# Query projection of the 16-head cross-attention as three fp16 passes, weights split on GpSimd

## The reference

```python
q = (text_hidden @ Wq).reshape(B, T_text, 16, 128).transpose(0, 2, 1, 3)
k = (vision_tokens @ Wk).reshape(B, T_vis, 8, 128).transpose(0, 2, 1, 3)
v = (vision_tokens @ Wv).reshape(B, T_vis, 8, 128).transpose(0, 2, 1, 3)
# k and v are repeated for the two heads of a group
scores = jnp.einsum('bhtd,bhsd->bhts', q, k) / scale
attn = jax.nn.softmax(jnp.where(mask, scores, -jnp.inf), axis=-1)
out = jnp.einsum('bhts,bhsd->bhtd', attn, v)  # then the heads side by side
return out @ Wo
```

## Time and profile before

| what | value |
|---|---|
| median of the runs | 1304.71 us (1302.49 to 1308.16) |
| the profiled execution's own time | 1302.72 us |
| its span | 1301.0 us |
| TensorE busy | 1152.5 us, 89% |
| VectorE busy | 994.7 us, 76% |
| ScalarE busy | 860.9 us, 66% |
| GpSimd busy | 315.3 us, 24% |
| the projection's matmuls (line 442) | 192 records |

### The profile page before, as it was taken

The page is one execution under the profiler, slowest core; times in us unless marked ns, Lnnn a source line. Parts: engine busy times, 40 slices in busy tenths (PEclk is TensorE's granted clock), DMA queues, the critical chain, the costliest instruction groups (busy, mean ns, idle before and its releaser), DMA issues. The chain is left out here.

```text
span 1301.0 us, 23119 instructions
## 1 busy us (share of the span) xinstructions
PE 1152.5 (89%) x8740; PEld 765.0 (59%) x8744; DVE 994.7 (76%) x1866; ACT 860.9 (66%) x1303; POOL 315.3 (24%) x353
## 2 busy tenths in 40 slices
PE   7999999848776887799899999887998999999997
PEld 3677767635322444486566666645874666666654
DVE  6887788197768883593889989776987998998654
ACT  5787778484454887332777777565876777777563
POOL 3000000100362000000172654502650456265100
PEclk8999999959986999899899999999998999999989
DMA  7999989201374000901899999614745999999600
GB/s 279 181 187 189 189 166 192 70 1 73 84 144 81 2 3 2 232 36 59 152 198 183 206 184 168 124 54 157 206 115 129 180 181 185 177 164 163 122 1 9
DMA packets 450833, 170.00 MB, mean 131 GB/s; under 512 B 437160, under 2 KB 437544, under 8 KB 449064
## 3 DMA queue, kind: packets, MB, share of 16 engines
q1 hardware_dynamic: 450736, 168.72, 62.3%
HBM read 58.84 MB, written 0.26 MB: 45 GB/s over the span
## 5 line engine op out<-in xcount | busy, mean ns | idle before, releaser
L462 PE MATMUL ps<-ctxT,L_xattn_qk 128*128 128x512 f16 x1152 | 269.4, 384 | 0.8 <-DVE L_xattn_mx L742 0.5
L766 DVE SCALAR_TENSOR_TENSOR arena<-L_xattn_sm,L_xattn_rr,arena 128x1024 f16<-128x1024 f32 x192 | 260.5, 1398 | 9.4 <-ACT arena L612 9.4
L597 ACT ACTIVATE L_xattn_sm<-L_xattn_sm,L_xattn_mx 128x2048 f32<-128x2048 f32 x96 | 192.3, 2003 | 74.9 <-DVE L_xattn_mx L742 73.5
L612 ACT ACTIVATE arena<-L_xattn_sm,L_xattn_rr 128x1024 f16<-128x1024 f32 x192 | 210.0, 1140 | 5.2
L462 PEld LDWEIGHTS ps<-ctxT,L_xattn_qk 128*128 128x128 f16 x1152 | 112.3, 99 | 129.4 <-issue 8.9
L484 PE MATMUL ps<-arena,ctx 128*128 128x256 f16 x1488 | 177.6, 273 | 0.0
L484 PEld LDWEIGHTS ps<-arena,ctx 128*128 128x128 f16 x1488 | 145.4, 98 | 31.9
L742 DVE CUSTOM_DVE_ANT_0 L_xattn_sm<-ps,L_xattn_bias 128x1024 f32<-128x1024 f32 x96 | 117.1, 1220 | 55.0 <-issue 54.7
L742 DVE CUSTOM_DVE_ANT_0 L_xattn_sm<-ps,L_xattn_bias,L_xattn_mx 128x1024 f32<-128x1024 f32 x96 | 123.2, 1284 | 2.0 <-DVE L_xattn_mx L742 1.3
L475 PE MATMUL ps<-arena,ctx 128*128 128x128 f16 x1488 | 100.8, 222 | 9.7 <-DMA arena<-arena 9.5
L475 PEld LDWEIGHTS ps<-arena,ctx 128*128 128x128 f16 x1488 | 92.3, 99 | 25.1 <-DMA arena<-arena 13.3
(11 more groups left out here) (586 smaller groups left out, 2094.2 us busy)
## 6 DMA issues: line engine op xcount, KB each, us to landing
L_ffn_ring<-in_L_ffn_experts SPq DMA_DIRECT2D x34, 384.0 KB, 3.7
arena<-in_L_xattn_w SPq DMA_DIRECT2D x36, 320.0 KB, 3.7
arena<-in_L_ffn_experts SPq DMA_DIRECT2D x8, 768.0 KB, 8.6
arena<-in_L_xattn_w SPq DMA_DIRECT2D x6, 640.0 KB, 8.5
arena<-arena SPq DMA_TRANSPOSE x193, 4.5
arena<-in_L_ffn_codes SPq DMA_DIRECT2D x1, 3072.0 KB, 12.2
arena<-in_L_attn_w SPq DMA_DIRECT2D x1, 2163.0 KB, 19.1
arena<-in_L_attn_w SPq DMA_DIRECT2D x2, 1026.0 KB, 5.0
```

Of the source, the lines that this page charges most:

```text
L462: last = nc.tensor.matmul(ps[:, at, :], qk[:, h // 2, qp, h % 2, b * P:(b + 1) * P], k.ctxT[:, cp, b, at * 512:(at + 1) * 512], start=(a = ...
L597: nc.scalar.activation(sm[:, u % 2, :], sm[:, u % 2, :], ACT.Exp, bias=mx[:, u % 2, 1:2], scale=-1.0, accum_out=rs[:, u % 2:u % 2 + 1]).th ...
L612: nc.scalar.mul(pp[:, u % 2, 0, at], sm[:, u % 2, at], rr[:, u % 2:u % 2 + 1]).then_inc(s.p_high, 1)
L766: nc.vector.scalar_tensor_tensor(pp[:, u % 2, 1, at], sm[:, u % 2, at], rr[:, u % 2:u % 2 + 1], pp[:, u % 2, 0, at], ALU.mult, ALU.subtrac ...
```

## The change

The query projection of the three layers is computed in three fp16 passes. Its two factors are split:

- The norm. ScalarE copies the turned norm from PSUM as fp16 (the high part), then VectorE subtracts that from PSUM into a second fp16 tile (the low part). Both lie in the memory of `k.xnT`, as `xh`. TensorE waits for the low part (`xn_low`).
- The weights. GpSimd copies a group's Wq to fp16 and subtracts (`split_queries`), into a new tile `wqh` with two places. TensorE waits for `wq_low` where it waited for the load. The wait for the load moves to GpSimd, which also waits until the projection that last read the place is done.

`q_project` issues 12 matmuls instead of 4. In L0_xattn GpSimd splits the first two groups around its subtractions and all others after them, as their weights arrive. In L2_xattn and L3_xattn it splits groups (0, 0) and (0, 1) before the first expert; the split of (i+1, 0) stands between the scalings and the clips of expert i, that of (i+1, 1) behind the clips.

The diff, without its first hunk, which adds the semaphore `xn_low`:

```diff
--- before.py
+++ after.py
@@ -302,7 +302,7 @@
             return stack.enter_context(nc.sbuf_tensor(f"{name}_{nm}", shape, dt))
         s = semaphores(nc, stack, name, "wq0 wq1 wv0 wv1 out_done qT_psum qT_ready qk_psum qk_high qk_ready s_ready "
                  "s_read0 s_read1 p_ready r_raw r_ready p_high p_low t_hi0 t_hi1 t_lo0 t_lo1 mixed "
-                 "oT_ready oh_psum oh_ready mask_ready last_psum last_hi last_lo0 last_lo1 oT_low", k.turns[slot])
+                 "oT_ready oh_psum oh_ready mask_ready last_psum last_hi last_lo0 last_lo1 oT_low wq_low", k.turns[slot])
         w = k.arena[slot][:, 0:2 * GW].rearrange("p (a n) -> p a n", a=2)
         bias = sb("bias", [P, B, CTX], BF16)
         anyone = sb("anyone", [P, B])
@@ -314,6 +314,8 @@
         pp = k.arena[slot][:, 2 * GW + 2 * CTX:2 * GW + 4 * CTX].bitcast(F16).rearrange("p (s a n) -> p s a n", s=2, a=2)
         pt = k.arena[slot][:, 2 * GW:2 * GW + 2 * CTX].bitcast(F16)\
             .rearrange("p (s a t q) -> p s a t q", s=2, t=KT, a=2)
+        xh = flat(k.xnT[:]).bitcast(F16).rearrange("p (a c t) -> p a c t", a=2, c=DC)
+        wqh = sb("wqh", [P, 2, 2, 2 * DC * HD], F16)
         qT = sb("qT", [P, 2, T])
         qk = sb("qk", [P, 2, 2, 2, T], F16)
         mx = sb("mx", [P, 2, 2])
@@ -326,7 +328,7 @@
             weigh = Weigh(sb("round", [P, WE]), sb("exp", [P, FE // 2, WE // BLK]), sb("inv", [P, FE // 2, WE // BLK]))
         oT = sb("oT", [P, T])
         oh = sb("oh", [P, T])
-        wq = [w[:, i, 0:2 * DC * HD].rearrange("p (h c d) -> p h c d", h=2, c=DC) for i in range(2)]
+        wq = [wqh[:, i, :, :].rearrange("p a (h c d) -> p a h c d", h=2, c=DC) for i in range(2)]
         wkT = [w[:, i, 512:640] for i in range(2)]
         wv = [w[:, i, 640:768] for i in range(2)]
         wo = [w[:, i, 768:768 + 2 * D].rearrange("p (h d) -> p h d", h=2) for i in range(2)]
@@ -425,22 +427,19 @@
                 keep_busy(k, 1, 3 if opening else 4, still)
                 xT_tensor(k, pe, k.xn, 0, n)
                 keep_busy(k, 1, 5, still)
-                pe.wait_ge(g.xnT_ready, k.xt + 1)
+                pe.wait_ge(g.xn_low, {"L0_xattn": 1, "L2_xattn": 2, "L3_xattn": 3}[name])
 
                 def q_project(i, j, first):
 
-                    if first and opening:
-                        pe.wait_ge((g.first_w0, g.first_w1)[j], 16)
-                    elif first:
-                        wait_weights(k, pe, slot, loaded)
-                    else:
-                        pe.wait_ge(wq_sem[j], 16 * i)
+                    pe.wait_ge(s.wq_low, 2 * i + j + 1)
                     if not (first and j == 0):
                         pe.wait_ge(s.qk_ready, 2 * i + j)
                     for h in range(2):
                         for c in range(DC):
-                            last = nc.tensor.matmul(PREP[:, h * T:(h + 1) * T], wq[j][:, h, c, :], k.xnT[:, c, :],
-                                                    start=(c == 0), stop=(c == DC - 1))
+                            for a, (wpart, xp) in enumerate(PARTS):
+                                last = nc.tensor.matmul(PREP[:, h * T:(h + 1) * T], wq[j][:, wpart, h, c, :],
+                                                        xh[:, xp, c, :], start=(c == 0 and a == 0),
+                                                        stop=(c == DC - 1 and a == len(PARTS) - 1))
                     last.then_inc(s.qT_psum, 1)
 
                 def qk_project(i, j):
@@ -579,7 +578,8 @@
             @block.scalar
             def _(act):
                 ln_scalar(k, act, n)
-                xT_scalar(k, act, k.xnT, 0)
+                act.wait_ge(g.xnT_psum, k.xt + 1)
+                nc.scalar.copy(xh[:, 0, :, :].rearrange("p c t -> p (c t)"), ps[:, 0, :]).then_inc(g.xnT_ready, 1)
                 nc.scalar.activation(unused[:], k.zero[:], ACT.Exp, bias=k.zero[:])
 
                 def q_copy(i, j):
@@ -693,22 +693,48 @@
 
             @block.gpsimd
             def _(pool):
+                def split_queries(chain, i, j):
+
+                    if i == 0 and opening:
+                        pool.wait_ge((g.first_w0, g.first_w1)[j], 16)
+                    elif i == 0:
+                        wait_weights(k, pool, slot, loaded)
+                    else:
+                        pool.wait_ge(wq_sem[j], 16 * i)
+                        pool.wait_ge(s.qT_psum, 2 * i + j - 1)
+                    chain(nc.gpsimd.tensor_copy(wqh[:, j, 0, :], w[:, j, 0:2 * DC * HD]))
+                    nc.gpsimd.tensor_tensor(wqh[:, j, 1, :], w[:, j, 0:2 * DC * HD], wqh[:, j, 0, :], ALU.subtract)\
+                        .then_inc(s.wq_low, 1)
+
                 if opening:
                     constants_pool(k, pool)
+                chain = Chain(pool, g.pool_chain, k.pool_n)
+                split_queries(chain, 0, 0)
+                if opening:
                     for b, done in enumerate((g.values_high0, g.values_high1)):
+                        if b:
+                            split_queries(chain, 0, 1)
                         pool.wait_ge(done, 1)
                         for half in range(2):
                             at = slice(half * CTX // 2, (half + 1) * CTX // 2)
                             nc.gpsimd.tensor_tensor(rows_of(1, b)[:, at], raw_context(k, b)[1][:, at], rows_of(0, b)[:, at],
                                                     ALU.subtract).then_inc(g.values_low, 1)
-                if experts is not None:
-                    experts_pool(k, pool, weigh, experts)
+                    for i in range(1, LASTI + 1):
+                        for j in range(2):
+                            split_queries(chain, i, j)
+                else:
+                    split_queries(chain, 0, 1)
+                    experts_pool(k, pool, chain, weigh, experts, split_queries)
+                k.pool_n = chain.n
 
             @block.vector
             def _(dve):
                 if opening:
                     dve.wait_ge(g.x_loaded, 16)
                 ln_vector(k, dve, k.x, k.xn, LN_EPS, n)
+                dve.wait_ge(g.xnT_ready, k.xt + 1)
+                nc.vector.tensor_tensor(xh[:, 1, :, :].rearrange("p c t -> p (c t)"), ps[:, 0, :],
+                                        xh[:, 0, :, :].rearrange("p c t -> p (c t)"), ALU.subtract).then_inc(g.xn_low, 1)
                 if opening:
                     dve.wait_ge(g.mask_loaded, 16)
                 else:
@@ -3200,10 +3226,9 @@
     k.dve_n = chain.n
 
 
-def experts_pool(k, pool, w, first):
+def experts_pool(k, pool, chain, w, first, split_queries):
 
     nc, g = k.nc, k.g
-    chain = Chain(pool, g.pool_chain, k.pool_n)
     blocks = WE // PIECES // BLK
 
     for e in range(first, first + FE // 2):
@@ -3216,11 +3241,15 @@
         for j in range(PIECES):
             nc.gpsimd.tensor_tensor(in_blocks(y[j]), in_blocks(y[j]), each_block(inv[j]), ALU.mult)\
                 .then_inc(g.w_scaled, 1)
+        if e % 4 < LASTI:
+            split_queries(chain, e % 4 + 1, 0)
         pool.wait_ge(g.w_bits, e + 1)
         for j in range(PIECES):
             nc.gpsimd.tensor_scalar(y[j], y[j], E4M3_TOP, -E4M3_TOP, ALU.min, ALU.max)
             last = nc.gpsimd.tensor_scalar(r[j], r[j], E4M3_LOW, ROUND, ALU.max, ALU.mult)
         chain(last)
+        if e % 4 < LASTI:
+            split_queries(chain, e % 4 + 1, 1)
         shared = e % 4 == 3
         if shared:
             for j in range(PIECES // 2, PIECES):
@@ -3235,7 +3264,6 @@
         for j in own:
             nc.gpsimd.tensor_tensor(in_blocks(coded[j]), in_blocks(y[j]), each_block(ex[j]), ALU.mult)\
                 .then_inc(g.w_coded, 1)
-    k.pool_n = chain.n
 
 
 def turn_experts(k, sp, own):
```

More of the change, by code:

```diff
@@ L104, in begin @@
                                "keys_high0 keys_high1 keys_low0 keys_low1 values_high0 values_high1 values_low const_id const_zero const_ones const_copied "
-                               "var_ready std_ready xn_ready xnT_psum xnT_ready dve_chain act_chain pool_chain "
+                               "var_ready std_ready xn_ready xnT_psum xnT_ready xn_low dve_chain act_chain pool_chain "
                                "w_loaded0 w_loaded1 out_stored ln_chain "
```

## The result

The changed kernel took 1363.8 us (median of 4 runs, 1360.2 to 1367.8) against 1304.5 us before: 1.045 times as long, with a 95% interval of 1.041 to 1.050. Forecast were 1355 us, in a range of 1330 to 1370. The profiled execution took 1360.2 us, its span is 1358.4 against 1301.0, 57.4 us more.

The account below looks back on a forecast made before the run. TensorE was taken to bound the loops. From 1302.7 us: projections -8.5, starts +0.5, stalls +23.6 and +10.0, port +12.0, clock +13.0 gave 1353.3; 2.0 for the median made it 1355 us, range 1330 to 1370.

Parts of the forecast that it names:

- Stalls, 33.6 us bare: L2 and L3 loops: TensorE waits for GpSimd's queued weight splits, 23.6 us over six u = 2 and 10.0 over six u = 6.
- The port, 12.0 us: L2 and L3: VectorE's operations beside GpSimd's splits lengthen each of 12 splits by 1.0 us through shared SBUF access.
- the first place: TensorE's u = 2 in L2 and L3, where the split queued behind GpSimd's scalings was forecast 3.4 to 4.0 us late.
- rival A: L2 and L3: bare stalls, splits at their median times and the clock staying up; 1330 us, chance 0.20.
- The clock, 13.0 us: L2 and L3: TensorE's clock drops behind the six long stalls at u = 2, costing 2.16 us each.
- Rival B: L2 and L3: the clock also falls behind the stalls at u = 6, another 13.0 us; 1368 us, chance 0.20.
- second places: TensorE's u = 6 in L2 and L3, where the split queued behind GpSimd's clips was forecast about 1.7 us late.
- Projections, -8.5 us: Loops of the three layers: twelve fp16 matmuls replace four fp32 ones, saving 0.47 us in each of 18 projections.
- The starts, +0.5 us: Start of L2 and L3: VectorE's added norm subtraction, less the shorter matmuls, costs +0.27 us in each layer.
- L0's second split: Start of L0: GpSimd's second split ends near 26.0, about when TensorE arrives; a lag of tenths would be harmless.
- Rival C: L2 and L3: a backlogged VectorE catches up during stalls, which vanish from 5 us of backlog; 1296.7 us, chance 0.05.

Follow-up runs that it names:

- the filled stalls: Changed kernel plus 18 unread 512-column matmuls on TensorE ahead of the projection at u = 2 in L2 and L3: 1354.9 us, ratio 1.0372.
- run 14: Not a run label: the verb in "could run 14 and 18 us earlier". Changed kernel with both splits ahead of their waits: 1309.0 us.

## Why the prediction was right, point by point

- **Stalls, 33.6 us bare.** Right at both places. The test was to set the end of GpSimd's scalings and clips against TensorE's arrival. Less 1.0 us each for the port, the stalls at u = 2 are 4.3 us in the first bodies and 3.7 in the others, on average 3.9 as forecast. By body there is one miss over 0.3 us: for the first of L2 the forecast was 3.4, from scalings of 3.20 us, and they took 4.18 in the changed kernel.
- **The port, 12.0 us.** Right: 45.2 us of stalls measured against 45.6, with the extra 1.0 us on the copy at the first place and mainly on the subtraction at the second, each beside VectorE's pair. That this pair is the cause is read from the timeline; no run took it away. The copies' own median would have given rival A; the clip's maximum, taken beside VectorE's pair, was the nearer row.
- **The clock, 13.0 us.** 10.8 us at the first places, by the filled stalls, and 1.7 us each behind two of the short ones (680.51 to 686.10 against 743.54 to 747.45): 14.2 in all. That the mean of two samples fitted is partly luck: it was 2.8 us in the two first bodies and 1.3 in the four others. Rival B's fall at all second places came only with the filler.
- **Projections, -8.5 us.** This term was mis-sized where nothing stalls. 0.47 us each is right in L0, six times. In L2 and L3 without stalls the intervals shrank by 0.2 us or less in most bodies, because VectorE holds TensorE back there. In the changed kernel the error hardly shows: a stall lets VectorE catch up, and the twelve intervals of the two layers grew by 52.8 us together, against 45.6 + 13.0 - 5.6 = 53.0 from my terms and 45.2 + 14.2 - 5.6 = 53.8 from the measured ones.
- **The starts, +0.5 us.** The term that failed. I counted VectorE's subtraction and called the first splits hidden, since GpSimd had nothing else to do. They ran beside VectorE's norm. From the block's start to the first scores L2 took 10.90 us instead of 9.27 and L3 12.08 instead of 9.27: +4.4, of which 3.1 are the slower norm (1.55 twice) and 1.2 is L3's low clock there.
- **L0's second split.** Forecast some tenths late and harmless; it was 1.16 us late. GpSimd's two subtractions took 5.20 us instead of 4.66: the first of the four is longer than the others (3.04 us already before the change), which their mean of 2.33 hid. And TensorE came 0.5 us earlier than before. It was harmless within tenths: from the first to the third projection L0 took 39.7 us instead of 39.4.
- **Rival C**, VectorE catching up, has a grain: the interval from u = 6 to u = 2 of the first bodies grew by 5.4 us in L2 and 5.7 in L3, where stall, clock and the shorter projection add up to 4.73 + 1.68 - 0.47 = 5.9. In L2's next body it grew by 4.27 us for 4.73 - 0.47 = 4.26. Over the twelve intervals 1.0 us is missing, not the 5 us of backlog that the rival needed. That VectorE's catching up is what gave it back is an inference.

L2 and L3 together: 45.2 + 14.2 + 4.4 = 63.8, less 55.2 measured, leaves 8.6 us given back, 5.6 by the shorter projections; the other 3.0 are the 1.0 above and 2.0 outside the loops' intervals, which aren't traced to a cause. With L0's -2.3 that is 52.9 of the span's 57.4; the other 4.5 are in untouched layers and differ from profile to profile.

The sum came out better than its terms. The forecast was 50.6 us more in the profiled execution, measured were 57.4. Of the 6.8 between them 4.5 are the untouched layers, 0.5 is L0, and 1.7 are left in L2 and L3, where the starts (+3.9), the clock (+1.2) and the stalls (-0.4) met 3.0 us given back that no term had.

## What to carry to other kernels

When a product's input gets a new producer, find the place in the producer's list and ask what the instructions ahead of it wait for; the splits could run 14 and 18 us earlier and stood behind waits that had nothing to do with them. Moving them ahead of those waits gave back 55 of 59 us. And a saving on the busiest engine is only worth its microseconds where no other engine holds it back: a projection gave back all its 0.47 us in L0, with VectorE busy 49.26 of 60 us, and 0.2 us or less in most bodies of L2 and L3, with 54.02 of 60.

## What was not expected of the hardware

- A GpSimd operation holds up even a tiny VectorE one: 0.17 us became 0.78 for two columns. It began at 604.11, inside GpSimd's subtraction, and ended at 604.89, just behind that one's end (603.71 + 1.15 = 604.86). That VectorE operation has one SBUF tensor as input. The Trainium skill ("GPSIMD Engine Reference", 1. Specifications) names VectorE instructions with two SBUF inputs or in a 2-port mode; the runs don't show which of the two applies here.
- The same short stall of 2.62 us left the clock at 1.00 four times in the changed kernel and brought it down six times of six once the long stalls were filled; with the first split early, and no long stalls at all, it did so three times of six. Which of the two comes out isn't told by the length of the idle time alone.
- Layers with unchanged instructions come near one of two lengths in most profiles (20.6 or 23.3 us in one layer, 50.6 or 53 in another, 55.6 or 59 in the last), about 3 us apart; what decides between them wasn't looked into. That is why differences of 3 us between variants are not settled here by single profiles.
